# Softmax sums spread by transfers inside SBUF, and one half of the scan's decay moved from PSUM to SBUF

## The reference

```
xn = layernorm(h) * w + b
attn = softmax(causal(q k^T / sqrt(8))) v @ o_w + o_b          # 16 heads of 8 channels
h_t  = exp(dt_t * A) * h_(t-1) + (x_t * dt_t) * B_t            # state-space scan, 256 channels x 16 states
y_t  = sum_n C_t[n] h_t[n];  ssm = ((y + x_c * D) * silu(z)) @ ssm_out_w
x    = x + alpha * attn + (1 - alpha) * ssm
```

## Time and profile before

| what | us |
|---|---|
| median of 3 runs | 1673.72 |
| lowest and highest of them | 1668.92, 1680.34 |
| the profiled execution | 1669.76 |
| its span in the profile | 1668.0 |
| busy over the span: PE, DVE, ACT, POOL | 1408.5, 1261.6, 1093.5, 863.4 |
| first and last scan | 123.6, 835.4 |

### The profile page before, as it was taken

How to read it: one execution, slowest core, us unless ns; L and a number is a source line. 1 busy time by engine, 2 the same in 40 slices (tenths; PEclk the granted TensorE clock), 3 DMA queues, 4 the chain that set the end, 5 groups by cost and what they waited for, 6 DMA issues and landing times. The chain is left out here.

```text
span 1668.0 us, 22123 instructions
## 1 busy us (share of the span) xinstructions
PE 1408.5 (84%) x7164; PEld 884.0 (53%) x7164; DVE 1261.6 (76%) x1873; ACT 1093.5 (66%) x1864; POOL 863.4 (52%) x889
## 2 busy tenths in 40 slices
PE   3688898888989898887767887999999999868687
PEld 3234444444444444444324645787786877725573
DVE  2149999989798988989915858687686767848857
ACT  2475668686767778786746736777878788621017
POOL 3137677778696978878843113022222222248843
PEclk9787899999999999999988989999999999979889
DMA  3112222222222222222003010111111111000001
GB/s 90 45 39 83 77 63 78 80 75 70 64 68 67 78 73 68 80 76 75 27 1 95 19 48 26 33 48 45 40 49 39 45 45 45 26 0 1 0 1 50
DMA packets 61688, 84.73 MB, mean 51 GB/s; under 512 B 6621, under 2 KB 32071, under 8 KB 61575
## 3 DMA queue, kind: packets, MB, share of 16 engines
q1 hardware_dynamic: 61474, 83.30, 16.0%
q10 hardware_dynamic: 100, 0.03, 0.0%
HBM read 74.38 MB, written 8.78 MB: 50 GB/s over the span
## 5 line engine op out<-in xcount | busy, mean ns | idle before, releaser
L1760 POOL TENSOR_TENSOR dBx<-dtx,Bb 128x512 f32<-128x512 f32 x256 | 319.6, 1272 | 11.4 <-DMA Bb<-b_dram 10.1
L1355 DVE TENSOR_TENSOR hl<-lsq,hh 128x512 fp32r<-128x512 f32 x320 | 259.5, 821 | 86.7 <-ACT hh L1644 78.9
L1325 DVE TENSOR_TENSOR_SCAN hy<-bank,dBx 128x512 f32<-128x512 f32 x256 | 297.8, 1203 | 10.5 <-ACT bank L1628 6.0
L1641 ACT ACTIVATE lsq<-bank,vcol 128x512 f32<-128x512 f32 x320 | 219.4, 692 | 108.1 <-DVE hl L1355 61.0
L1050 PE MATMUL bank<-QK 127*128 127x128 bf16 (+7 forms) x1024 | 237.7, 318 | 46.6 <-DVE Mx L1315 27.9
L1315 DVE TENSOR_REDUCE Mx<-bank 128x1 f32<-128x384 f32 (+3 forms) x352 | 212.1, 627 | 57.5 <-PE bank L1050 56.7
L1784 POOL TENSOR_TENSOR stage<-stage,lrs 128x512 f32<-128x512 f32 x64 | 92.3, 1443 | 310.5 <-DVE lrs L1435 310.5
L1050 PE MATMUL bank<-x,we1h 128*128 128x512 f32 x640 | 210.7, 411 | 18.8 <-DVE x L1343 9.4
L1569 ACT ACTIVATE PT<-bank 128x512 f32<-128x512 f32 x320 | 183.7, 596 | 52.9 <-PE bank L1050 51.3
L1628 ACT ACTIVATE bank<-dtv,alog 128x512 f32<-128x512 f32 x256 | 170.4, 692 | 61.2 <-DVE hy L1325 60.8
L1050 PEld LDWEIGHTS bank<-QK 127*128 127x128 bf16 (+1 forms) x1024 | 94.3, 104 | 191.9 <-issue 51.5
(11 more groups left out here) (258 smaller groups left out, 2393.6 us busy)
## 6 DMA issues: line engine op xcount, KB each, us to landing
Bb<-b_dram SPq DMA_DIRECT2D x128, 256.0 KB, 3.6
stage<-w_rows SPq DMA_DIRECT2D x64, 256.0 KB, 3.2
parts<-part SPq DMA_DIRECT2D x16, 384.0 KB, 2.7
QK<-parts SPq DMA_DIRECT2D x64, 96.0 KB
QK<-parts SPq DMA_DIRECT2D x64, 64.0 KB
stage<-in_L_ffn_We_dram SPq DMA_DIRECT2D x16, 256.0 KB, 3.3
hy<-in_L_attn_x_dram SPq DMA_DIRECT2D x8, 256.0 KB, 5.8
QK<-parts SPq DMA_DIRECT2D x64, 32.0 KB
```

The source lines that it names most:

```text
L1325: engine.tensor_tensor_scan(hst[:, 2 * (g % 3) + h, :], bank[4 + h][:], dBx[:, g % 4, h, :], 0.0, ALU.mult, ALU.add).then_inc(sems["dve_sc ...
L1355: engine.tensor_tensor(hl[:, sl, :], full[:, f, :], hh[:, sl, :].bitcast(F32), ALU.subtract).then_inc(sems["dve_hl"], 1)
L1641: engine.activation(full[:, f, :], o[:], fn, bias=bias).then_inc(sems["act_up"], 1)
L1760: engine.tensor_tensor(dBx[:, sl, h], dtx[:, b % 2, h], Bb[:, sl], ALU.mult).then_inc(sems["pool_dbx"], 1)
```

## The change

The sums are spread by 8 DMA transfers inside SBUF instead of by a matmul with `seld`, which goes with its four set-up instructions. For each group of 32 rows, one transfer writes row 8 of `Os` to rows 0 to 8 of `rdn`, and one writes row 17 to rows 9 to 31. They are a step `sums` of their own, one piece behind `os`; `on` comes five pieces later, and `wo` four pieces after that. The logarithm works in place in `rdn`. `On` is used with one of its two buffers only. The other one is `dec`, the decay of the first half of the channels, so that the scans of that half read both inputs from SBUF; those of the second half read bank 5 as before. Bank 4 joins the ring, and is taken out of it while the first norms run.

```diff
-    ring = [0, 1, 2, 6, 7]
+    ring = [0, 1, 2, 4, 6, 7]
...
-        yield
-        k = take()
-        it = step("on", b=b, g=g, o1=o1, bank=k, free=free.get(f"b{k}"), lrs_free=free.get(f"lrs{hf}"), on_free=free.get(f"On{hf}"))
-        it["m"] = up("pe_dn")
-        it["e1"] = free[f"b{k}"] = up("act_dn")
-        it["e2"] = up("act_dn")
+        it = step("sums", g=g, o1=o1, lrs_free=free.get(f"lrs{hf}"))
+        d = it["d"] = up(f"sum_in{hf}", 128)
+        for _ in range(5):
+            yield
+        it = step("on", b=b, g=g, d=d, on_free=free.get("On"))
+        it["e1"], it["e2"] = up("act_dn"), up("act_dn")
...
-        it = step("decay", g=g, dt=ssm[b]["dt"], free=[free.get(f"b{4 + h}") for h in range(2)])
+        it = step("decay", g=g, dt=ssm[b]["dt"], free=(free.get("dec"), free.get("b5")))
...
-    for k in (0, 1, 2):
+    for k in (0, 1, 2, 4):
         ring.remove(k)
...
+        dec = On[:, 1, :]
...
-                elif kind == "on":
-                    q.wait_ge(("pool_set", pool_set["sel"]), it["o1"], it["free"])
-                    mm(o[:], seld[:], Os[:]).then_inc(sems["pe_dn"], 1)
...
-                        engine.tensor_tensor_scan(hst[:, 2 * (g % 3) + h, :], bank[4 + h][:], dBx[:, g % 4, h, :], 0.0,
+                        engine.tensor_tensor_scan(hst[:, 2 * (g % 3) + h, :], bank[5][:] if h else dec, dBx[:, g % 4, h, :], 0.0,
...
-                    q.wait_ge(it["m"], it["lrs_free"])
-                    engine.activation(t, o[:], ACT.Ln).then_inc(sems["act_dn"], 1)
+                    q.wait_ge(it["d"])
+                    engine.activation(t, t, ACT.Ln).then_inc(sems["act_dn"], 1)
...
-                        engine.activation(bank[4 + h][:], dtv[:, b % 2, h, :], ACT.Exp,
+                        engine.activation(bank[5][:] if h else dec, dtv[:, b % 2, h, :], ACT.Exp,
...
+                elif kind == "sums":
+                    hf = it["g"] // 2
+                    q.wait_ge(it["o1"], it["lrs_free"])
+                    for i in range(4):
+                        for r0, r1, row in ((0, 9, 8), (9, 32, 17)):
+                            src = Os[32 * i + row:32 * i + row + 1, :].rearrange("p (o t) -> p o t", o=1).broadcast_to([1, r1 - r0, T])
+                            engine.dma_start(rdn[32 * i + r0:32 * i + r1, hf, :], src).then_inc(sems[f"sum_in{hf}"], 16)
```

More of the change, by code:

```diff
@@ L253, in normalise @@
         it = step("wo", b=b, g=g, bank=k, free=free.get(f"b{k}"), on=on, h=h_last[b] or r_n[b])
-        it["m"] = free[f"On{hf}"] = up("pe_wo")
+        it["m"] = free["On"] = up("pe_wo")
         it["hd"] = free.get("hd")
@@ L379, in scan @@
         for h in range(2):
-            free[f"b{4 + h}"] = free[f"dBx{g % 4}{h}"] = it["x"][h]
+            free[("dec", "b5")[h]] = free[f"dBx{g % 4}{h}"] = it["x"][h]
     def accumulate(g):
@@ L487, in plan_mixers @@
     fetch(0)
-    for k in (0, 1, 2):
+    for k in (0, 1, 2, 4):
         ring.remove(k)
     run_together(p.norms(first_norms([(1, 1)] + [(b, l) for l in range(2) for b in range(2, NB)])), 12, (mixer, 5, False))
-    ring.extend((0, 1, 2))
+    ring.extend((0, 1, 2, 4))
     fetch(1)
@@ L862, in build @@
         identb = sb("identb", [P, P], BF16)
-        seld = sb("seld", [P, P])
         epsc = sb("epsc", [P, 1])
@@ L1001, in on_set @@
             return {name: i + 1 for i, name in enumerate(names.split())}
-        pool_set = on_set("vrow qk0 qk1 qk2 qk3 wo id0 id om cm on ep mask0 mask idb idn sel0 sel1 sel2 sel bsum vb0 mr vb qz0 qz1 qz2")
+        pool_set = on_set("vrow qk0 qk1 qk2 qk3 wo id0 id om cm on ep mask0 mask idb idn bsum vb0 mr vb qz0 qz1 qz2")
         dve_set = on_set("row0 row1 sc0 sc1 neg abs sgn2 max sgn gate om1 av2 av3 A qbs")
@@ L1124, in tensor_program @@
                     x.then_inc(sems["pe_av"], 1)
-                elif kind == "on":
-                    q.wait_ge(("pool_set", pool_set["sel"]), it["o1"], it["free"])
-                    mm(o[:], seld[:], Os[:]).then_inc(sems["pe_dn"], 1)
                 elif kind == "wo":
                     q.wait_ge(("ld_wo", 128), it["on"], it["free"])
-                    mm(o[:], wo[:, it["g"] // 2, :], On[:, it["g"] // 2, :]).then_inc(sems["pe_wo"], 1)
+                    mm(o[:], wo[:, it["g"] // 2, :], On[:, 0, :]).then_inc(sems["pe_wo"], 1)
                 elif kind == "taps":
@@ L1712, in gpsimd_program @@
             engine.tensor_scalar(identn[:], ident[:], -1.0, None, ALU.mult).then_inc(sems["pool_set"], 1)
[L1713 to L1718, removed]
             engine.memset(bsum[:], 0.0).then_inc(sems["pool_set"], 1)
@@ L1744, in gpsimd_program @@
                     q.wait_ge(it["e2"], it["on_free"])
-                    engine.tensor_tensor(On[:, hf, :], Os[:], rdn[:, hf, :], ALU.mult).then_inc(sems["pool_on"], 1)
+                    engine.tensor_tensor(On[:, 0, :], Os[:], rdn[:, hf, :], ALU.mult).then_inc(sems["pool_on"], 1)
                 elif kind in ("wo", "so"):
```

## The result

The changed kernel is slower: 1739.69 us (median of 4 runs, 1737.46 to 1741.79) against 1671.78 for the kernel before beside it. The ratio is 1.0397, with a 95% interval of 1.0356 to 1.0439, so +68 us. The profiled execution has a span of 1738.0 us.

A forecast was written before the change was run, and what follows sets the result against it. DVE, busy 90.8% of the 720 us mixers, was taken as nearest to a bound. 1669.8 + 41 (decay and bank) + 5.6 (tail) = 1716.4 us, and 3.9 from profiled run to median made 1720; range 1655 to 1762.

The forecast's parts named there:

- My term of 54 us of waiting for DVE: Mixers: 128 scans each wait 0.42 us on average for POOL's instruction, raising DVE's demand from 654 to 708 us.
- POOL's share: Mixers: POOL can't read while the 128 scans run, 154 us, so its demand rises from 554 to 708 us.
- the efficiency: Mixers: DVE's share of the stretch, taken to rise from 90.8% to 93%, making the stretch 761 us.
- the bank: Mixers: a sixth bank cuts waits of PE and DVE, taken as DVE's share rising from 90.8% to 93%.
- 708 / 0.908: Mixers: the bound with DVE's demand of 708 us at today's share of 90.8%, +60 us.
- A fill of 98%: Mixers: the bound if both DVE and POOL could be filled to 98%, given as +3 us.
- the term of +41 for decay and bank together: Mixers: DVE's 708 us at 93% make the stretch 761 us in place of 720, containing the bank's gain.
- the transfers are hidden beside scores and scans with 2 to 4 us to spare: Mixers: issue and landing of the sums, 6.4 to 8.4 us, fit within 10.7 us before the logarithm.
- My third rival: Mixers: SP stands for dBx, sums land up to 5 us late, +45 us on the forecast, 1765 us; chance 0.08.
- the tail: Last step, nothing beside it: 1.2 us between Os and logarithm become 6.8, +5.6 us once (bounds 4.2 and 8.4).
- The signs that I had named: Profile after: scans 1.5 to 1.8 us, maxima above 2.4; DVE, POOL over 90%; PE's waits shrink; tail about 7 us.
- The two other rivals: Mixers: the lock mostly hides, 1681 us, chance 0.12; or a scan doesn't contend with POOL, 1648 us, chance 0.15.

The follow-up runs named there:

- e3: Against the kernel before: first half's decay in SBUF, bank 4 left unused (five banks), sums by the matmul; 1711.49 us, ratio 1.0236.
- e5: Against e3: first half's decay in SBUF for every second state only, in bank 4 for the others; 1727.63 us, ratio 1.0323.
- e1: The change without its transfers: sums by the matmul, first half's decay in SBUF, bank 4 in the ring; 1696.46 us, ratio 1.0143.
- e6: Kernel before with the sums by transfers (five banks, decays in PSUM) and the Q and K fetch one piece later; 1733.25 us, ratio 1.0374.
- e7: Kernel before with the sums by transfers, but by the matmul for the last sequence; five banks, decays in PSUM; 1689.44 us, ratio 1.0097.
- e9: Against e7: logarithm nine pieces behind the issue of the transfers in place of five; 1683.28 us, ratio 1.0072 to the kernel before.
- e10: Against e9: first half's decay in SBUF and bank 4 in the ring added; 1711.60 us, ratio 1.0217 to the kernel before.
- e8: Against e6: the last sequence's sums by the matmul again, as in e7; 1712.52 us, ratio 1.0246 to the kernel before.

## Why the prediction was right or wrong

**Right: the place, the sign and the mechanism of the larger loss.** Scans with two SBUF inputs contend with POOL, and e3 puts this at +41 us. My term of 54 us of waiting for DVE measured 47 ((1569 - 1203) x 128) in the changed kernel and 40 in e3. In these 55 to 59 of 128 scans meet no wait, where a random meeting with a POOL that is 77% busy would leave about 30; scans and POOL fall into step, by my reading. By the Trainium skill (SBUF — State Buffer, section "SBUF: two separate sides") whichever of the two starts first has the ports for its whole instruction, and the other blocks. For the scan the timeline agrees, 1.60 us at 234.37 and POOL's pair at 3.43. e5 goes beyond what the page says: one POOL instruction that is inside is not all that a scan may wait for.

**Wrong in size: POOL's share and the efficiency.** I charged POOL the whole 154 us. Its busy time rose by 649.25 - 553.59 = 96; the rest fell into its idle time. Without the bank my working gave 708 / 0.908, +60 us; e3 measured +41, at 692.7 / 757.3 = 91.5% of DVE. For the bank I had 19 us and e1 measured 15. With it e1's DVE reached 697.1 / 739.9 = 94.2%, over my 93%. (A fill of 98% gives 708 / 0.98 = 722, +2, which my bounds have as +3.) So the term of +41 for decay and bank together was really +26 us.

**Wrong: "the transfers are hidden beside scores and scans with 2 to 4 us to spare".** This step failed. The issue took 5.8 to 7.0 us for eight in place of 4.8. SP was still issuing the fetch for 2.2 to 3.6 us after `Os` in seven steps. And in the 13 steps in which ACT stood, the logarithm started 6.6 to 9.5 us behind the last issue, where I had 1.6 to 3.6 for the landing. This last is the largest of the three, and it is there also in the six of the 13 steps in which SP began with the sums as soon as `Os` was ready. My working had SP's waits in it, but not what SP issues just ahead of this step, though the twelve transfers of the fetch stood in my own rows; with the fetch behind the sums (e6) the landing is 3.5 us. My third rival had the effect, late sums and ACT's standing (29.7 us in 13 steps), but not this way to it: it had SP stand for dBx. e7 puts it at +15 us. In the profiles e9 cuts the mixers' part from 15.7 us to 5.1.

**Wrong in size: the tail.** +16.1 us in place of +5.6. The plan's last two sums lie in the tail, not one. The first makes ACT stand for 7.4 us. The second takes 10.3 in place of 1.2, not 6.8: issue 7.0, landing 3.3.

**Why the sum was near.** By luck: -15 us of error on the decay and +15 on the sums in the mixers cancel. Left are +10.5 in the tail and some 10 us that no part alone shows. The parts measured alone give 1.43 + 1.93 = 3.36%, the whole 3.97%; the 0.6% between them are about as much as the three intervals together leave open (an estimate: 0.58%). In the profiles' mixers the parts add to 20.5 + 16.3 = 36.8 us, and the whole has 51.4. With the sums repaired they add to 25.6, and e10 has 34.7. So the halves seem to make each other worse, but the timed runs can't show it, and what would do it is open.

**The signs that I had named.** These held: the long scans' median of 1582 ns beside 1.19 us for those with a bank, dBx at up to 2292 ns, DVE over 90%, PE's share down from 84.9% to 77.6, ACT's waits for scans up from 60.9 us to 69.4 + 24.4. These didn't: the longest scan stayed under 2.4 us (2319 ns), POOL was busy for 84.3% and not over 90, PE's waits for the maxima rose to 58.7 us, and the tail shows 10.4 and 10.3 us between `Os` and the logarithm in place of 7.

The two other rivals fell. The contention didn't hide behind other work: e1's ratio is clear of 1. And the first-half scan didn't keep its 1.2 us beside POOL.

## What to carry to other kernels

When a DVE operand moves from PSUM to SBUF, count the DVE instructions that then have two SBUF inputs and look up how busy POOL is beside them: here 128 scans beside a POOL that is 77% busy cost 41 us, more than the PSUM bank gained (15 us). When a matmul is replaced by transfers, lay the issue time, the landing and what the queue has in front on the timeline against the place of use, for every instance and for the last ones apart, where nothing runs beside them.

## What the runs showed that I had not expected

- A DVE scan kept out by POOL isn't always let in at POOL's next boundary: in e5 it stood through six more instructions, up to 5.66 us. It happened to 4 of 64 scans, a fifth took 3.68 us, and none of 128 took over 2.32 us in the kernels with twice as many.
- The fifth bank of the ring is worth 52 us where PE's visible wait for banks was 35 us: by my reading a wait in PE's order moves DVE's, ACT's and POOL's work too.
- Eight transfers of 18 and 46 KB inside SBUF take 0.76 us each to issue (median, 599 to 1041 ns), though the nearest row had 0.60, and as long on ACT's queue (0.77).
- The unchanged stages behind the first next norm take 787.4 us after and 783.6 before. The difference goes with a stretch between DVE's last `hl` of the experts and its first product of the band stage (the columns of the earlier trace rows), before and after:

```profile
1452.10:1474.80 22.70, 16.93 (x41) 6.83 (x39) 5.64 (x13) 6.56 (x23) 6.04 (x4) 0.85 0.00 1
1516.00:1544.80 28.80, 23.03 (x36) 8.58 (x34) 5.59 (x12) 5.44 (x19) 6.04 (x4) 0.56 0.00 1
```

It is 28.8 us at a granted clock of 0.56, near the lower of the clock's two levels (1.2 of 2.4 GHz), in place of 22.7 us at 0.85. All the variants have some 28.8 us there, but for e6 (25.6) and e8 (22.7, at 0.85 again). So up to 6 us of the other profiles' difference from the kernel before go with the clock in a stretch that no edit touched, and the stretches of the mixers and the tail are compared without it. Why the clock falls there is open.
